# Feed-forward stage of a transformer layer on eight cores: weight blocks transposed one step ahead of their matmuls, and a down projection in 512 columns with a barrier in its loop

## The chip, the cores and the metric

The kernel runs on the 8 cores of one Trainium2 chip. The metric is the device time in microseconds (us) of the slowest core. The cores don't exchange anything: each has its own 1024 tokens and reads all weights itself.

## The reference

One transformer layer, pre-norm, on 8192 tokens of width 4096. The attention half has 32 query heads of 128 and one shared key and value head:

```python
def _silu(x):
    return jax.nn.silu(x)
def attn(x, wq, wk, wv, wo):          # x: 1 x 8192 x 4096
    q = (x @ wq).reshape(B, T, 32, 128)
    k = x @ wk
    v = x @ wv
    probs = softmax(causal(q @ k.T * scale))
    return (probs @ v).reshape(B, T, C) @ wo
def ffn(x, w_gate, s_gate, w_up, s_up, w_down, s_down):
    g = jnp.einsum('th,ih->ti', xt, w_gate.astype(x.dtype)) * s_gate   # i = 11008
    u = jnp.einsum('th,ih->ti', xt, w_up.astype(x.dtype)) * s_up
    h = jax.nn.silu(g) * u
    return jnp.einsum('ti,hi->th', h, w_down.astype(x.dtype)) * s_down
x = x + attn(layernorm(x), ...)
x = x + ffn(layernorm(x), ...)
```

The three feed-forward weights are int32 tables with values of -127 to 127, one scale for each row.

## The kernel before

A core owns eight tiles of 128 tokens (`OWN` = 1024 columns). It computes keys and values of all 64 tiles, its own queries, attention, the output projection with wo (line 645), the residual, and the second layer norm, whose transposed result lies in SBUF as `BUF`: 32 chunks of the hidden dimension, each 128 partitions by 1024 tokens. Then come the two stages that the change touches.

**F1, the gate and up projections (lines 695 to 785).** The inner dimension of 11008 is worked in `NI` = 86 blocks of 128. For each block the three weights (`mi` 0 gate, 1 up, 2 down) come in four pieces of 128 x 1024 (`cg`). For every piece:
- POOL issues a DMA that casts int32 to bf16 (`ldw`, line 716), into one of two buffers that each weight has for itself, `wbf_in[mi][cg % 2]`. It waits until the piece two before it of the same weight is transposed.
- TensorE transposes its eight 128 x 128 squares into one of two PSUM tiles, `pb` (line 723).
- VectorE copies that tile to SBUF (line 734), and frees it.
- For gate and up, TensorE multiplies at once by the eight chunks of `BUF`, in two halves of 512 tokens: 16 matmuls (line 749). Gate sums up in ps_a and up in ps_b. A down piece has no matmul: its transpose is only stored.

So TensorE has, in a row: transposes of a piece, a wait for their copy, 16 matmuls of that piece, transposes of the next. At the end of a block, one SyncE DMA stores the transposed down weight of 128 x 4096 in the DRAM tensor `wdt_s` (line 756), ScalarE does silu (762), VectorE multiplies (767) and copies the first 256 tokens to `h_res` (777), and the other 768 go to the DRAM tensor `h_sp` (783).

**F2, the down projection (lines 789 to 863).** The 1024 tokens are four groups of 256 (`GT`), worked in two passes of two groups. In a pass, for each of `NJ` = 32 output chunks, SyncE loads a strip of the transposed down weight, 128 x 86 x 128, in pieces of 256 bytes (line 816), into one of two buffers; it waits for the matmuls of two strips before. For each of the two groups come 86 matmuls of 256 columns (829), a scaling from PSUM (835), and for each of two token tiles: a transpose (844), a load of the residual `y_sp` by POOL (849), an addition (853) and a store of the output by POOL (858). POOL's queue is in order, and load and store alternate on it: the load of a tile's residual stands behind the store of the tile before. A strip has four such tiles in all, and the whole stage 256.

**What orders the work.** Each engine gets its instructions in the order in which the program adds them. `Prog` (lines 31 to 116) turns each dependency into a wait on a semaphore. `P.barrier` (line 51) adds a NO_OP on all five engines (line 113 in the trace) that waits for the last instruction of each engine and for the last DMA of each stream. In this kernel barriers stand only between stages, "endF1" and "final" among them.

Of the kernel before, what the change touches and what calls it, by code (L numbers as in the profile page):

```python
# [118 lines left out]
def build_nc(T=8192, I_FFN=11008):  # L119
# [5 lines left out]
    NG = max(1, OWN // 256)  # L125
    GT = OWN // NG
# [3 lines left out]
    def nch(p):  # L130
# [21 lines left out]
    d_hsp = (nc.dram_tensor("h_sp", [NI, 128, OWN - GT], BF16).ap()  # L152
             if NG > 1 else None)
# [6 lines left out]
    with ExitStack() as stk:  # L160
# [20 lines left out]
        def stat(slot):  # L181
# [521 lines left out]
        hres_cp = None  # L703
        for i in range(NI):
            ipar = i % 2
            gu_last = [[None] * NHALF, [None] * NHALF]
            wdtcgs = []
            for mi, dw in enumerate((d_wg, d_wu, d_wd)):
                for cg in range(4):
                    wpar = cg % 2  # L710
                    if mi < 2:
                        src = dw[i * 128:(i + 1) * 128, cg * 1024:(cg + 1) * 1024]
                    else:
                        src = dw.rearrange("(j q) c -> q j c", q=128)[
                            :, cg * 8:(cg + 1) * 8, i * 128:(i + 1) * 128]
                    ldw = dma("gp", wbf_in[mi][wpar], src,
                              deps=[win_rel.get((mi, wpar))], tag="wld",
                              stream=f"wl{mi}{wpar}")
                    pbp = (cg + mi) % 2
                    trs = []  # L720
                    for s in range(8):
                        trs.append(add("t", lambda e, s=s, mi=mi, wpar=wpar,
# [80 lines left out]
        for ipass, gset in enumerate(passes):  # L803
            hbuf = {}
            hloads = []
            for k, g in enumerate(gset):
                tgt = h_res if k == 0 else h_2nd
                hbuf[g] = tgt
                if ipass == 0 and k == 0:
                    continue  # L810
# [144 lines left out]
```

How the kernel before makes its waits and increments, by code:

```python
        def run_engine(handle, eng):  # L83
# [11 lines left out]
                    if (p["eng"] == eng and e_["fn"] is not None  # L95
                            and e_["sem"] == p["sem"]):
                        pass
                    sname = p["sem"]
                    if satisfied.get(sname, 0) >= p["val"]:
                        continue
                    waits[sname] = max(waits.get(sname, 0), p["val"])
                if eng in CHAIN_ENGS and prev_val is not None:
                    waits[eng] = max(waits.get(eng, 0), prev_val)
                for se, v in sorted(waits.items()):
                    handle.wait_ge(get_sem(se), v)
                    satisfied[se] = v
                if e_["fn"] is not None:
                    inst = e_["fn"](handle)
                    if e_["val"] is not None:
                        inst.then_inc(get_sem(e_["sem"]),
                                      16 if e_["sem"].startswith("D:") else 1)
                elif e_["val"] is not None:
                    handle.nop().then_inc(get_sem(e_["sem"]), 1)
```

## Time and profile before

| | us |
|---|---|
| median of 2 runs | 13707.56 |
| the two runs | 13509.33 and 13905.8 |
| the profiled execution, time | 13509.33 |
| its span, slowest core (core 1) | 13507.8 |
| spans of the eight cores | 13362.5 to 13507.8 |

The profiled execution is the faster of the two runs; 1.5 us of its time lie outside the span. The trace is that of core 1. F1 lies from 6762 to 11305 us of the span and F2 from 11305 to its end. PE is TensorE's matmuls (a transpose is one of them), PEld its weight loads, DVE VectorE, ACT ScalarE, SP SyncE.

### The profile page before, as it was taken

The numbers are of one execution on the slowest core, as the hardware profiler recorded it, in microseconds if no ns is written. First come the engines' busy times: TensorE is split into PE (matmuls) and PEld (weight loads), VectorE is DVE, ScalarE is ACT, GpSimd is POOL, SyncE is SP. The second block draws the span as 40 slices with busy tenths as digits, with TensorE's granted clock in tenths as the row PEclk, the third lists the DMA queues.
The fourth block names the chain that finished last, engine by engine and source line by source line (L and its number), as shares of the span: only waits on it lengthen the run. The fifth ranks groups of instructions, "written<-read, shape, count | busy, mean of one in ns | idle before, by whom it ended". The sixth has DMA issues, their size and how long they took to land.

```text
span 13507.8 us, 161305 instructions; the slowest of 8 cores (13362.5 to 13507.8 us)
## 1 busy us (share of the span) xinstructions
PE 8560.6 (63%) x62528; PEld 5506.4 (41%) x62528; DVE 4714.6 (35%) x8140; ACT 2398.4 (18%) x3696; POOL 1069.6 (8%) x1649
## 2 busy tenths in 40 slices
PE   3444675555655555678477777777767765665766
PEld 3443234444444444433233333333333333554655
DVE  4443117877777777720311111111111111000000
ACT  3443003444444444400100000000000000000000
POOL 0000000000000000000011111111111111111111
PEclk6666887888888888888588888888888888887888
DMA  3223660000000000067455555555555555544444
GB/s 119 113 113 112 106 106 1 1 1 1 1 1 1 1 1 1 1 72 91 145 86 81 82 86 82 81 86 81 82 86 81 82 85 104 107 101 113 103 103 96
DMA packets 1471353, 944.14 MB, mean 70 GB/s; under 512 B 1229296, under 2 KB 1338736, under 8 KB 1448336
## 3 DMA queue, kind: packets, MB, share of 16 engines
q0 software_dynamic: 683760, 423.86, 24.5%
q1 hardware_dynamic: 786848, 509.97, 12.4%
q8 instruction: 514, 8.42, 0.3%
q14 instruction: 231, 1.89, 0.1%
HBM read 1149.57 MB, written 157.42 MB: 97 GB/s over the span
## 4 chain that ended last, share of the span: by engine, by line
PE 41%; DMA 22%; DVE 21%; issue 8%; ACT 6%; POOL 1%; DVEq 1%; ACTq 0%; POOLq 0%; SPq 0%; PEldq 0%
DMA AR<-y_sp 12%; PE ps_a L749 11%; PE ps_b L749 9%; DVE AR L505 6%; DMA AR<-wd 4%; DVE AR L734 4%; PE pb L723 3%; ACT AR L518 3%; DVE AR L261 3%; PE pb L544 3%; PE ps_b L476 2%; ACT AR L276 2%; DMA AR<-wq 2%; PE pf_b L581 2%; PE pb L292 2%
## 5 line engine op out<-in xcount | busy, mean ns | idle before, releaser
L734 DVE COPY AR<-pb 128x1024 bf16<-128x1024 bf16 x1032 | 705.1, 690 | 3754.3 <-PE pb L723 3754.1
L749 PE MATMUL ps_a<-AR 128*128 128x512 bf16 x5504 | 1424.7, 418 | 386.4 <-DVE AR L734 386.4
L749 PE MATMUL ps_b<-AR 128*128 128x512 bf16 x5504 | 1243.0, 379 | 324.8 <-DVE AR L734 324.8
L476 PE MATMUL ps_b<-AR 128*128 128x512 bf16 x1152 | 428.4, 460 | 1107.8 <-ACT AR L518 632.0
L723 PE MATMUL pb<-AR 128*128 128x128 bf16 x8256 | 719.0, 241 | 607.1 <-DMA AR<-wd 549.8
L749 PEld LDWEIGHTS ps_a<-AR 128*128 128x128 bf16 x5504 | 555.9, 105 | 1153.0 <-issue 688.0
L544 PEld LDWEIGHTS pb<-AR 128*128 128x128 bf16 x9216 | 779.4, 116 | 435.6 <-issue 272.1
L723 PEld LDWEIGHTS pb<-AR 128*128 128x128 bf16 x8256 | 603.3, 108 | 822.7 <-issue 660.4
L292 PE MATMUL pb<-AR 128*128 128x128 bf16 x2560 | 292.8, 304 | 988.0 <-ACT AR L276 980.5
L544 PE MATMUL pb<-AR 128*128 128x128 bf16 x9216 | 889.1, 253 | 28.7 <-ACT AR L518 23.1
L762 ACT ACTIVATE AR<-ps_a,AR 128x512 f32<-128x512 f32 x172 | 118.2, 688 | 4419.4 <-PE ps_a L749 4330.9
L749 PEld LDWEIGHTS ps_b<-AR 128*128 128x128 bf16 x5504 | 513.7, 97 | 944.1 <-issue 374.5
L564 DVE COPY AR<-pb 128x1024 bf16<-128x1024 bf16 x1152 | 787.3, 683 | 1.2 <-issue 1.2
L476 PE MATMUL ps_a<-AR 128*128 128x512 bf16 x1152 | 440.0, 471 | 472.1 <-ACT AR L518 294.4
L829 PE MATMUL ps_b<-AR 128*128 128x256 bf16 x5504 | 735.2, 304 | 0.0
L829 PE MATMUL ps_a<-AR 128*128 128x256 bf16 x5504 | 645.1, 281 | 131.2 <-DMA AR<-h_sp 76.8
L292 PEld LDWEIGHTS pb<-AR 128*128 128x128 bf16 x2560 | 250.6, 138 | 1027.4 <-issue 1021.0
L829 PEld LDWEIGHTS ps_b<-AR 128*128 128x128 bf16 x5504 | 605.0, 110 | 125.0
L829 PEld LDWEIGHTS ps_a<-AR 128*128 128x128 bf16 x5504 | 556.0, 101 | 210.2 <-issue 131.6
L518 ACT ACTIVATE AR<-ps_a,AR 128x1024 bf16<-128x1024 f32 x576 | 632.4, 1098 | 1.3 <-issue 0.7
L518 ACT ACTIVATE AR<-ps_b,AR 128x1024 bf16<-128x1024 f32 x576 | 632.4, 1098 | 1.3 <-issue 1.1
L505 DVE TENSOR_REDUCE AR<-ps_b 128x1 f32<-128x1024 f32 x512 | 624.6, 1220 | 20.7 <-PE pb L544 1.5
(89 smaller groups left out, 9376.2 us busy)
## 6 DMA issues: line engine op xcount, KB each, us to landing
AR<-wdt_s SPq DMA_DIRECT2D x64, 2752.0 KB, 22.3
AR<-x SPq DMA_DIRECT2D x64, 2048.0 KB, 8.4
AR<-wg POOLq DMA_DIRECT2D x344, 256.0 KB, 6.4
AR<-wu POOLq DMA_DIRECT2D x344, 256.0 KB, 5.0
AR<-wd POOLq DMA_DIRECT2D x344, 256.0 KB, 5.8
wdt_s<-AR SPq DMA_DIRECT2D x86, 1024.0 KB, 4.0
AR<-wq POOLq DMA_DIRECT2D x64, 1024.0 KB, 9.6
AR<-xq SPq DMA_DIRECT2D x16, 2048.0 KB, 11.9
```

What stands on the lines that cost most here:

```text
L261: e1 = add("v", lambda e: e.reduce_sum(s_sum, src, axis=AX.X), deps_in, "ln_sum")
L276: e9 = add("s", lambda e: e.activation(dst_bf, src, AF.Identity, bias=s_negmr, scale=s_rstd), [e8], "ln_apply")
L292: e.transpose(p[:, s * 128:(s + 1) * 128], src_bf[:, j * 128:(j + 1) * 128], eye16),
L476: e.matmul(S[:, sh * 512:(sh + 1) * 512], BUF[:, h * OWN + p * 128: h * OWN + (p + 1) * 128], KT[:, n * 1024 + sh * 512: n * 1024 + (sh + ...
L505: rmx = add("v", lambda e, S=S, ph=ph: e.reduce_max(mtmp[ph], S[:, :], axis=AX.X, negate=True), ms_after + [mneg_last.get(ph)], "rmax")
L518: eev = add("s", lambda e, S=S, cp=cp, ph=ph: e.activation(p_sb[cp], S[:, :], AF.Exp, bias=mneg[ph]), ms_after + [bias_ready, p_rel.get(cp ...
L544: trs.append(add("t", lambda e, s=s, cp=cp: e.transpose(pb_t[cp][:, s * 128:(s + 1) * 128], p_sb[cp][:, s * 128:(s + 1) * 128], eye16), [r ...
L564: ptev = add("v", lambda e, cp=cp: e.tensor_copy(pt_sb[cp], pb_t[cp][:, :]), r["trs"] + [pts_rel.get(cp)], "ptev")
L723: pbp=pbp: e.transpose(pb_t[pbp][:, s * 128:(s + 1) * 128], wbf_in[mi][wpar][:, s * 128:(s + 1) * 128], eye16),
L734: tev = add("v", lambda e, dst=dst, pbp=pbp: e.tensor_copy(dst, pb_t[pbp][:, :]), trs + xd, "wtev")
L749: half=half, hp=hp: e.matmul(psg[mi][hp][:, 0:HT], wT[mi][wpar][:, s * 128:(s + 1) * 128], BUF[:, j * OWN + half * HT: j * OWN + (half + 1 ...
L829: e.matmul(psd[gp_], strip[sp][:, i * 128:(i + 1) * 128], hb[:, i * GT:(i + 1) * GT], start=(i == 0), stop=(i == NI - 1)), dep, "dmm")
```

## The change

Three things are done; nothing is changed ahead of F1.

1. **F1.** A piece's 16 matmuls are not added right behind its transposes but put in a list (`pending`), and are added once the next gate or up piece has been transposed. The work at a block's end (silu, multiply, copies, store) goes through the same list. The last up piece's matmuls therefore stand behind the four down pieces of transposes. The six input buffers, two for each weight, become four that all pieces go through in turn; the transposed pieces too have four. The transposed down weight is stored in four DMAs of 128 x 1024 out of two buffers, where it was one of 128 x 4096.
2. **F2.** A pass works one group of `GTP` = 512 tokens: 86 matmuls of 512 columns for a strip where there were twice 86 of 256. The number of strips, 64, and of token tiles, 256, stays. The second pass loads its 512 columns of `h_sp` in one DMA on SyncE's queue, where POOL loaded three parts of 256.
3. **The barrier "final"** has moved into the loop over the output chunks `j`: it is added 64 times, at the end of each.

```diff
-        for i in range(NI):
+        for i_ffn in range(NI):
...
-                    wpar = cg % 2
+                    buf = ub % 4
+                    ub += 1
...
-                    ldw = dma("gp", wbf_in[mi][wpar], src,
-                              deps=[win_rel.get((mi, wpar))], tag="wld",
-                              stream=f"wl{mi}{wpar}")
-                    pbp = (cg + mi) % 2
+                    ldw = dma("gp", wbf_in[buf], wsrc,
+                              deps=[win_rel.get(buf)], tag="wld",
+                              stream=f"wl{buf}")
+                    pbp = buf % 2
...
+                    if mi == 2:
+                        wd_dma = dma("sy", d_wdt[i, :, cg * 1024:(cg + 1) * 1024],
+                                     wdtcg[cg % 2], deps=[tev],
+                                     tag="wdtout", stream=f"wd{cg % 2}")
+                        wdt_rel[cg % 2] = wd_dma
                         continue
...
+                    def mk_mm(i=i, mi=mi, cg=cg, buf=buf, tev=tev,
+                              gu_last=gu_last):
...
+                    pending.append(mk_mm())
+                    flush()
...
-            wdt_dma = dma("sy", d_wdt[i], wdt_full[ipar], deps=wdtcgs,
-                          tag="wdtout", stream=f"wd{ipar}")
...
+            pending.append(mk_epi())
+            flush()
+        flush(0)
...
-        psd = [ps_a[:, 0:GT], ps_b[:, 0:GT]]
+        psd = [ps_a[:, 0:GTP], ps_b[:, 0:GTP]]
...
+        for ipass in range(NPASS):
+            hload = None
+            if ipass > 0:
+                hsrc = d_hsp.rearrange("i q c -> q i c")[
+                    :, :, (ipass - 1) * GTP: ipass * GTP]
+                hload = dma("sy", h_all, hsrc, deps=[pass_last], tag="hl",
+                            stream="hl")
             for j in range(NJ):
...
+                gp_ = j % 2
+                mm = None
+                for i in range(NI):
...
+                        psd[gp_], strip[sp][:, i * 128:(i + 1) * 128],
+                        h_all[:, i * GTP:(i + 1) * GTP],
+                        start=(i == 0), stop=(i == NI - 1)), dep, "dmm")
...
+                d_rel[gp_] = last_tr
+
+                P.barrier("final")
-        P.barrier("final")
```

`flush()` takes items from the head of `pending` and adds them until one is left.

How the instructions stand now. First TensorE in F1, from the third up piece of a block to the first gate pieces of the next. pb0 and pb1 are the two PSUM tiles of the transposes, ps_a and ps_b the sums of gate and up; x16 are the 16 matmuls of a piece. Before:

```order
L723 MATMUL pb1<-AR 128x128 x8
L749 MATMUL ps_b<-AR 128x512 x16
L723 MATMUL pb0<-AR 128x128 x8
L749 MATMUL ps_b<-AR 128x512 x16
L723 MATMUL pb0<-AR 128x128 x8
L723 MATMUL pb1<-AR 128x128 x8
L723 MATMUL pb0<-AR 128x128 x8
L723 MATMUL pb1<-AR 128x128 x8
L723 MATMUL pb0<-AR 128x128 x8
L749 MATMUL ps_a<-AR 128x512 x16
L723 MATMUL pb1<-AR 128x128 x8
L749 MATMUL ps_a<-AR 128x512 x16
```

The same place after the change:

```order
L731 MATMUL pb0<-AR 128x128 x8
L766 MATMUL ps_b<-AR 128x512 x16
L731 MATMUL pb1<-AR 128x128 x8
L766 MATMUL ps_b<-AR 128x512 x16
L731 MATMUL pb0<-AR 128x128 x8
L731 MATMUL pb1<-AR 128x128 x8
L731 MATMUL pb0<-AR 128x128 x8
L731 MATMUL pb1<-AR 128x128 x8
L766 MATMUL ps_b<-AR 128x512 x16
L731 MATMUL pb0<-AR 128x128 x8
L731 MATMUL pb1<-AR 128x128 x8
L766 MATMUL ps_a<-AR 128x512 x16
```

Each x16 row now belongs to the piece transposed one x8 row earlier than the row ahead of it, and the last of ps_b has moved behind the four down pieces.

Next TensorE in F2, one strip. st0 and st1 are the semaphores of the strip loads, sem_v VectorE's. Before:

```order
L829 MATMUL ps_a<-AR 128x256 [waits sem_D_sy_st0]
L829 MATMUL ps_a<-AR 128x256 x85
L844 MATMUL pf_a<-AR 128x128 [waits sem_v]
L844 MATMUL pf_b<-AR 128x128
L829 MATMUL ps_b<-AR 128x256 x86
L844 MATMUL pf_a<-AR 128x128 [waits sem_v]
L844 MATMUL pf_b<-AR 128x128
```

After, with the barrier's NO_OP; ow and yl are the semaphores of the output stores and of the residual loads:

```order
L847 MATMUL ps_a<-AR 128x512 [waits sem_D_sy_st0]
L847 MATMUL ps_a<-AR 128x512 x85
L862 MATMUL pf_a<-AR 128x128 [waits sem_v]
L862 MATMUL pf_b<-AR 128x128
L862 MATMUL pf_a<-AR 128x128 [waits sem_v]
L862 MATMUL pf_b<-AR 128x128 [waits sem_v]
L113 NO_OP [waits sem_D_gp_ow0,sem_D_gp_ow1,sem_D_gp_yl0,sem_D_gp_yl1,sem_s,sem_v]
```

One group of matmuls is left for a strip, four transposes follow it, and TensorE then waits until the last output store has landed.

Last SyncE, from the end of F1 into F2. Before:

```order
L240 DMA wdt_s<-AR 128x4096 [waits sem_D_sy_wd1,sem_v]
L240 DMA h_sp<-AR 128x768 [waits sem_D_sy_hs1,sem_v]
L113 NO_OP [waits sem_D_gp_wl00,sem_D_gp_wl01,sem_D_gp_wl10,sem_D_gp_wl11,sem_D_gp_wl20,sem_D_gp_wl21,sem_D_sy_hs0,sem_D_sy_hs1,sem_D_sy_wd0,sem_D_sy_wd1,sem_s,sem_t,sem_v]
L240 DMA AR<-wdt_s 128x86x128 x2
L240 DMA AR<-wdt_s 128x86x128 [waits sem_D_sy_st0,sem_t]
L240 DMA AR<-wdt_s 128x86x128 [waits sem_D_sy_st1,sem_t]
```

After:

```order
L239 DMA wdt_s<-AR 128x1024 [waits sem_D_sy_wd1,sem_v]
L239 DMA h_sp<-AR 128x512 [waits sem_D_sy_hs1,sem_v]
L113 NO_OP [waits sem_D_gp_wl0,sem_D_gp_wl1,sem_D_gp_wl2,sem_D_gp_wl3,sem_D_sy_hs0,sem_D_sy_hs1,sem_D_sy_wd0,sem_D_sy_wd1,sem_s,sem_t,sem_v]
L239 DMA AR<-wdt_s 128x86x128
L113 NO_OP [waits sem_D_gp_ow0,sem_D_gp_ow1,sem_D_gp_yl0,sem_D_gp_yl1,sem_D_sy_st0,sem_s,sem_t,sem_v]
L239 DMA AR<-wdt_s 128x86x128
L113 NO_OP [waits sem_D_gp_ow0,sem_D_gp_ow1,sem_D_gp_yl0,sem_D_gp_yl1,sem_D_sy_st1,sem_s,sem_t,sem_v]
```

Two strips were in hand at a time. Now the load of each strip stands behind a NO_OP that waits for everything of the strip before it.

## Rows read from the trace of the kernel before

**Rows 1.** The page's chain of waits: shares of the span by line.
```profile
DMA AR<-y_sp 12%; PE ps_a L749 11%; PE ps_b L749 9%; DVE AR L505 6%; DMA AR<-wd 4%; DVE AR L734 4%; PE pb L723 3%; ACT AR L518 3%; DVE AR L261 3%; PE pb L544 3%; PE ps_b L476 2%; ACT AR L276 2%; DMA AR<-wq 2%; PE pf_b L581 2%; PE pb L292 2%
```
**Rows 2.** Busy time in stretches: F1, then F2; the columns in the first line.
```profile
core 1: us, PE busy (x) PEld busy (x) DVE busy (x) ACT busy (x) POOL busy (x), PEclk, DMA share, GB/s
6762.00:11305.00 4543.00, 3236.94 (x19040) 1653.57 (x19040) 823.25 (x1279) 116.97 (x170) 662.88 (x1018) 0.88 0.53 83
...
11305.00:13508.00 2203.00, 1426.37 (x11264) 1189.78 (x11264) 129.25 (x384) 0.00 (x0) 284.56 (x515) 0.80 0.48 106
```
**Rows 3.** The waits in F1: who waited for whom, total us, times, longest.
```profile
PE pb L723 <- DMA AR<-wd: 544.0, 162, 7.1
PE ps_a L749 <- DVE AR L734: 382.6, 340, 2.0
...
PE ps_b L749 <- DVE AR L734: 321.1, 340, 0.9
```
**Rows 4.** Timeline of one block of F1: start, us, instruction, idle before it.
```profile
9007.48 6.24 PE L749 MATMUL ps_a<-AR 128*128 128x512 bf16 x16 [1.71 <-DVE AR L734]
...
9015.11 3.61 PE L749 MATMUL ps_a<-AR 128*128 128x512 bf16 x16 [0.94 <-DVE AR L734]
...
9018.56 0.61 PE L723 MATMUL pb<-AR 128*128 128x128 bf16 x8
...
9049.74 1.75 POOL L240 DMA_DIRECT2D AR<-wd  x2 [12.71 <-PE pb L723]
...
9054.77 1.01 PE L723 MATMUL pb<-AR 128*128 128x128 bf16 x8 [5.13 <-DMA AR<-wd]
```
**Rows 5.** The page's DMA issues: KB each, median us from issue to landing.
```profile
AR<-wdt_s SPq DMA_DIRECT2D x64, 2752.0 KB, 22.3
...
wdt_s<-AR SPq DMA_DIRECT2D x86, 1024.0 KB, 4.0
...
out<-AR POOLq DMA_DIRECT2D x256, 64.0 KB, 3.7
```
**Rows 6.** Timeline of F2: its first strip, then one residual load to the next.
```profile
11351.76 12.47 PE L829 MATMUL ps_a<-AR 128*128 128x256 bf16 x86 [54.42 <-DMA AR<-wdt_s]
11364.34 0.48 DVE L835 TENSOR_SCALAR AR<-ps_a,AR 128x256 f32<-128x256 f32 x1 [64.56 <-PE ps_a L829]
...
11365.22 9.55 PE L829 MATMUL ps_b<-AR 128*128 128x256 bf16 x86
...
11365.38 0.29 DVE L853 TENSOR_TENSOR AR<-pf_a,AR 128x128 f32<-128x128 f32 x1 [0.56 <-PE pf_b L844]
...
11856.56 0.29 DVE L853 TENSOR_TENSOR AR<-pf_a,AR 128x128 f32<-128x128 f32 x1 [5.81 <-DMA AR<-y_sp]
11857.42 0.54 POOL L240 DMA_DIRECT2D out<-AR  x1 [5.42 <-DVE AR L853]
11857.96 0.54 POOL L240 DMA_DIRECT2D AR<-y_sp  x1
11861.76 0.29 DVE L853 TENSOR_TENSOR AR<-pf_b,AR 128x128 f32<-128x128 f32 x1 [4.91 <-DMA AR<-y_sp]
```
**Rows 7.** All instructions on y_sp in F2: us to landing.
```profile
DMA to landing us min/median/max: 2.0/5.2/37.1
```
**Rows 8.** Busy time in 4 us of F2 while a strip is loaded.
```profile
11840.00:11844.00 4.00, 3.55 (x33) 2.94 (x30) 0.00 (x0) 0.00 (x0) 0.00 (x0) 1.00 1.01 229
```
**Rows 9.** The chain of waits: one of the two h_sp loads before pass two.
```profile
12427.64 25.50 DMA AR<-h_sp
```
**Rows 10.** The chain in the wo projection: two groups of 32 matmuls.
```profile
6095.78 8.42 PE ps_b L645 x32
...
6249.14 7.07 PE ps_a L645 x32
```
**Rows 11.** Busy time in 80 us of it, core 1, then core 2.
```profile
6091.00:6171.00 80.00, 75.44 (x283) 30.43 (x281) 6.23 (x9) 0.00 (x0) 6.70 (x4) 0.80 0.86 91
...
6091.00:6171.00 80.00, 71.56 (x326) 31.95 (x331) 6.91 (x10) 0.00 (x0) 8.38 (x5) 1.00 0.95 108
```

More of the change, by code:

```diff
@@ L740, in build_nc, with mk_epi, emit @@
+                    pending.append(mk_mm())
+                    flush()
+            def mk_epi(i=i, ipar=ipar, gu_last=gu_last):
+                def emit():
+                    nonlocal_state = None
+                    hlast = None
                     for half in range(NHALF):
                         hp = half % 2
[L742 to L753 removed]
@@ L802, in build_nc @@
         pass_last = None
[L803 to L810, printed above, removed]
-                src = d_hsp.rearrange("i q c -> q i c")[
-                    :, :, (g - 1) * GT: g * GT]
-                hloads.append(dma("gp", tgt, src, deps=[pass_last], tag=f"hl{g}", stream="hl"))
+        for ipass in range(NPASS):
[5 more added lines that the diff above has]
+                            stream="hl")
             for j in range(NJ):
@@ new lines, in build_nc @@
+                strip_rel[sp] = mm
+                pass_last = mm
+                dev = add("v", lambda e, j=j, gp_=gp_: e.tensor_scalar_mul(
+                    dscr[gp_], psd[gp_], sd_sb[:, j:j + 1]),
+                    [mm, ld_sd, d_rel.get(gp_)], "dscl")
+                psd_rel[gp_] = dev
+                last_tr = None
+                for tt in range(GTP // 128):
+                    ptile = ipass * (GTP // 128) + tt
+                    fp = (j * (GTP // 128) + tt) % 2
+                    tr = add("t", lambda e, tt=tt, gp_=gp_, fp=fp:
+                             e.transpose(
+                        pf2[fp][:, 0:128],
+                        dscr[gp_][:, tt * 128:(tt + 1) * 128], eye32),
+                        [dev, ld_eye32, pf3_rel.get(fp)], "dtr")
+                    last_tr = tr
+                    yld = dma("gp", yscr[fp],
+                              d_ysp[ptile, :, j * 128:(j + 1) * 128],
+                              deps=[y_rel.get(fp)], tag="yld",
+                              stream=f"yl{fp}")
+                    oev = add("v", lambda e, fp=fp: e.tensor_tensor(
+                        oscr[fp], pf2[fp][:, 0:128], yscr[fp], ALU.add),
+                        [tr, yld, orel.get(fp)], "oadd")
+                    pf3_rel[fp] = oev
+                    y_rel[fp] = oev
+                    od = dma("gp", d_out[ptile, :, j * 128:(j + 1) * 128],
+                             oscr[fp], deps=[oev], tag="outw",
+                             stream=f"ow{fp}")
+                    orel[fp] = od
```

214 lines of the change are left out of this document (91 added, 123 removed).

## The prediction

> **What bounds the kernel now.** I read the chain of waits first, since the page's busy shares mix stages with different limits. Its costliest line is the residual load from y_sp in F2, 12% of the span, with the matmuls of F1 (L749) and its loads and copies (wd, L734) behind it [rows 1]. The change touches F1 and F2 alone, so I then took the two stretches: F1 is 4543 us, 52.8 for each of its 86 blocks, with TensorE busy 71%, and F2 is 2203 us, 34.4 for each of 64 strips [rows 2].
>
> In F1 the waits of TensorE name three things: down pieces that have not landed, 544.0 us; and VectorE's copy of the transposes ahead of the matmuls, 382.6 + 321.1 us [rows 3]. The timeline of one block shows both. After a piece's transposes TensorE idles 0.94 us until the copy is there, then works 3.61 us on 16 matmuls. Among the down pieces it idles 5.13 us for a load, and after that the first 16 matmuls take 6.24 us instead of 3.61: the granted clock is then at its lower level, half speed [rows 4].
>
> In F2 nothing on TensorE is the bound. The chain runs from one residual load to the next through POOL's queue. With little other traffic, one addition follows the last after 5.2 us (11856.56 to 11861.76) [rows 6]; four of these would be 21 us, but a strip takes 34.4, because the 64 KB transfers share the DMA engines with the strips: their landing ranges from 2.0 to 37.1 us [rows 7]. The strip's own 22.3 us [rows 5] lie beside this work today, since the next strip is always loaded ahead.
>
> **The change in F1.** With the transposes one piece ahead, the copy lies beside 16 matmuls and the 0.94 us wait goes, on all 8 pieces of a block. From the start of 16 matmuls to the next transposes are 3.45 us (9015.11 to 9018.56), and the transposes take 0.61 [rows 4]: 4.06 for a piece, 32.5 for eight. The four down pieces: 4 x 0.61 = 2.4, and 0.5 where the third and fourth wait for a copy, because there are two PSUM tiles. New is that the copy of the third down piece waits until the store of the first has landed, 4.0 us for 1 MB [rows 5], here 256 KB. Behind it stand the copies of the next gate pieces on VectorE. The last up piece's 3.45 us of matmuls cover most of that; I take 0.7 (bounds 0, if the small store lands in 2.5 us, and 4 if nothing covers it). Sum: 36.1 us a block, 3105 in all.
>
> Are the loads in time? A down piece lands 5.0 us after its issue (9049.74 to 9054.77) [rows 4]. The fourth is now issued once the last up piece is transposed. Then come 3.45 us of matmuls and three groups of transposes with their waits, some 6 us together. So it just lands in time, and the others earlier. The DMA engines were busy 0.53 of 52.8 us [rows 2], 28 us of work for a block; in 36.1 us that is 0.78. It fits, with little to spare. The cold start of 2.6 us for a block goes with the wait.
>
> Clock. All this is at the full clock, 1.00 or 2.4 GHz. The wo projection, where TensorE is as dense as F1 will be, shows another value: 0.80 on core 1 over 80 us, and in it 32 matmuls took 8.42 us instead of 7.07 [rows 10, 11]. It lies between the two levels of 1.2 and 2.4 GHz. Core 2 has 1.00 in the same 80 us [rows 11]. At that clock 16 matmuls are 4.2 us, a piece 4.95, a block 43.7, F1 3758 us. Nothing in the trace says how much of the new F1 will have it. I take half: 39.9 us a block, 3431 us. F1 then gains 1112 us, with bounds 785 and 1438.
>
> The Trainium skill (TensorE: Matmul & The Clock Gate, Part 1, the note on the peak-current limiter) says that a whole die goes to 13/16 of its clock once three of its cores run dense matmuls, and stays there while the load lasts. The trace differs in that core 1 had it and core 2 of its die did not [rows 11]. By the page all of F1 would be at 13/16, and the total would be that of the third case below.
>
> **The change in F2.** The matmul work stays: 86 x 512 columns for twice 86 x 256. What changes the stage is the barrier. SyncE's NO_OP waits for the last output store, and behind it stands the load of the next strip; TensorE's stands ahead of the next matmuls, POOL's ahead of the next residual load. The load, the matmuls and the four tiles, side by side before, now come one after the other. One round:
> - barrier and issue, 0.4 us (an estimate; signals between engines cost 0.1 to 0.6 in rows 6);
> - strip from issue to landing: 22.3 median [rows 5], with residual loads beside it. Alone I take 21.0;
> - matmuls: 3.45 / 16 = 0.216 us each, 18.7 for 86. After a round's wait the clock is at its lower level: 86 matmuls took 12.47 us after a long wait and 9.55 warm, 2.9 more [rows 6]. I take 2.5, so 21.2, and 0.2 to VectorE;
> - scaling of 512 columns: 0.48 for 256 [rows 6], at most 0.96, taken 0.8; transpose and hops up to the first addition 0.56 (11364.82 to 11365.38). Together 1.4;
> - three more tiles at 5.2 = 15.6. The first residual load lies beside the strip, the three others can't, since POOL's queue has each behind a store;
> - the last store is issued 0.9 us after its addition (11856.56 to 11857.42) [rows 6] and lands 3.0 later (3.7 median with strips beside it [rows 5]).
>
> Sum 63.7 us, 4077 for 64 rounds. The second pass's load of h_sp, twice what took 25.50 us [rows 9], stands ahead of a strip on the same queue: 50 more. F2 becomes 4127 us, 1924 longer. Bounds for a round: 54 (strip 16, tile cycle 4.0, cold start 1.5) and 74 (strip 25, tile cycle 7, last store 5), so F2 grows by 1300 to 2580.
>
> **Sum.** 13507.8 - 4543 + 3431 - 2203 + 4127 = 14319.8, and with the 1.5 us outside the span 14321; I say 14320. That is 6.0% over the profiled execution, 4.5% over the median, which holds a run of 13905.8. The time is meant against the undisturbed 13509.
>
> **Rivals.**
> *Full clock in F1.* Blocks of 36.1 us: 326 less, 13995. For it: in F1 before, the clock is 1.00 whenever it is warm. Against: rows 10 and 11.
> *F1 wins less: 0.81 throughout, or loads that come late.* The first gives 14321 + 327 = 14648. The second: four shared buffers leave the last down piece about 1 us of slack, with DMA engines at 0.78; if each block keeps its 5.13 us wait and the cold 2.6, that is 662 more than at full clock, 14657. The two prices are the same, so they are one case. Then the edit in F1 does only in part what it says.
> *Not slower: transfers alone run at their floor.* After the barrier no strip disturbs the residual loads, and they don't disturb the strip. In F2 the DMA engines reached 229 GB/s [rows 8]: at that rate 2.8 MB take 12.3 us, 14.5 with the ends, and a residual load lands in 2.0 instead of 3.8 [rows 7]. A round is shorter by 6.5 + 3 x 1.8 = 11.9 us, 762 in all: 13233 at full clock, 13559 at half. It decides the sign if a round is below 60.3 us at full clock, or 55.2 at half. Against: the load is made of 256-byte pieces and seldom reached this rate, and its 22.3 us are a median over rounds in which it was mostly alone with one small transfer.
> The Trainium skill (DMA: Bandwidth & Descriptors, Bandwidth) gives 6.15 us for 1 MB, and says in the same section that descriptors of 256 bytes lose speed to a fixed cost. By its rate the strip would be an estimated 17 us, which would take 4 us off a round. No row here shows a strip that fast.
>
> **How the numbers follow.** The forecast has 0.40, full clock in F1 0.25, little gain in F1 0.17, transfers at their floor 0.12, and 0.06 is left for rounds over 70 us. All but the fourth are slower; a measurement of this kernel can tell about 2% from no change, so up to 13780 counts as the same. Of the fourth I give 0.03 to faster and 0.09 to same, and 0.01 more to same for a round just under 60 us at full clock. Slower has 0.87. The range reaches from the middle of the fourth case, 13650, to 14950, which is past the third with rounds of 68 us.
>
> **What would show it.** F1's stretch at 3100 to 3760 us, no wait of L766 for VectorE's copy, almost none for wd. F2's at 4000 to 4250, with the wait of TensorE for wdt_s near 64 x 40 us (strip and tiles both lie in it), SyncE's queue waiting for out, and 16 us from the first to the last addition of a round. The chain should carry wdt_s as its largest DMA, which it does not hold today [rows 1]. I am wrong if a round is below 56 us, or if F1 stays above 3900.

## The result, and the profile after

| | before | after |
|---|---|---|
| median, us | 13649.45 (13 runs) | 14157.72 (14 runs) |
| lowest and highest | 13479.97, 13949.34 | 13771.96, 14408.9 |
| profiled execution | 13509.33 | 14094.02 |
| span of core 1 in it | 13507.8 | 13711.5 |

The changed kernel is slower: the ratio is 1.019, with a 95% interval of 1.010 to 1.028. So it is slower, but whether by more than 2% the interval leaves open. The sign and the range held, but the forecast said 6.0% over an undisturbed execution, and 1.9% was measured. In many executions the cores of one die show a lower granted clock and take 200 to 600 us longer; the ratio is taken without those, and so all stages below are read on core 1, whose die was not among the slow ones in either profiled execution.

The stages are cut alike in both traces: F1 from its first transpose to its last matmul, F2 from there to the end. Cut so, F1 of before begins at 6711 us and ends at 11289; the forecast was made from stretches that begin at 6762 and 11305, hence its 4543 and 2203 us where the table has 4578 and 2219.

| core 1, us | before | after | change | forecast |
|---|---|---|---|---|
| ahead of F1 | 6711 | 6571 | -140 | 0 |
| F1 | 4578 | 3372 | -1206 | -1112 |
| F2 | 2219 | 3769 | +1550 | +1924 |

The first row holds no edit. Cores 2 to 7 of before began F1 at 6592 to 6640 us, and over all profiled executions here cores began it at 6552 to 6740. The 140 us are thus a difference between two executions: core 1 began late in the one and early in the other. The forecast, which was made against the span of the first, took them along. Its error of 608 us on core 1 (14319.8 against 13711.5) is thus 140 + 94 from F1 + 374 from F2.

The chain of waits of the changed kernel (slowest core, 6), which answers to [rows 1]. wdt_s is now its largest DMA, y_sp has gone from 12% to 3%, and the store of wdt_s is new, with 4%:

```profile
PE ps_a L766 10%; DMA AR<-wdt_s 9%; PE ps_b L766 7%; DVE AR L504 6%; PE ps_b L847 5%; PE ps_a L847 5%; DMA wdt_s<-AR 4%; DMA AR<-y_sp 3%; PE pb L731 3%; ACT AR L517 3%; DVE AR L260 2%; PE pb L543 2%; PE ps_b L475 2%; ACT AR L275 2%; PE pf_b L580 2%
```

Busy time of the two stretches on core 1, against [rows 2]. In F1 TensorE went from 71% busy to 89% and its clock from 0.88 to 0.97. In F2 it went down to 38% of the stretch, at a clock of 0.67, and the DMA engines from 0.48 to 0.25. The stage moves nearly the same bytes in 1.7 times the time:

```profile
core 1: us, PE busy (x) PEld busy (x) DVE busy (x) ACT busy (x) POOL busy (x), PEclk, DMA share, GB/s
6572.00:9953.00 3381.00, 3000.16 (x19256) 1570.77 (x19256) 829.69 (x1290) 119.39 (x173) 668.07 (x1029) 0.97 0.77 111
9953.00:13711.00 3758.00, 1418.70 (x5760) 602.61 (x5760) 122.69 (x320) 0.00 (x0) 273.96 (x511) 0.67 0.25 60
```

**F1 after.** The waits of core 1 in F1, against [rows 3] (who waited for whom: us in total, times, longest):

```profile
DVE AR L742 <- DMA wdt_s<-AR: 546.8, 148, 8.4
PE pb L731 <- DVE AR L742: 273.2, 231, 4.8
PE pb L731 <- DMA AR<-wd: 85.7, 68, 3.3
...
PE ps_a L766 <- DVE AR L742: 3.1, 7, 0.5
```

The wait of the matmuls for VectorE's copy went from 703.7 us to 3.1, and that for down pieces from 544.0 to 85.7. In their place VectorE waits 546.8 us for stores of wdt_s, and TensorE's transposes 273.2 us for VectorE. The timeline of one block's end on core 1 shows how (start, us, instruction, idle before it):

```profile
8006.29 0.61 PE L731 MATMUL pb<-AR 128*128 128x128 bf16 x8
8006.73 3.62 PE L766 MATMUL ps_b<-AR 128*128 128x512 bf16 x16
...
8011.68 8.65 SPq L239 DMA_DIRECT2D wdt_s<-AR  x4
...
8012.81 3.62 PE L766 MATMUL ps_b<-AR 128*128 128x512 bf16 x16
...
8016.85 0.69 DVE L742 COPY AR<-pb 128x1024 bf16<-128x1024 bf16 x1 [4.66 <-DMA wdt_s<-AR]
8017.68 0.61 PE L731 MATMUL pb<-AR 128*128 128x128 bf16 x8 [1.25 <-DVE AR L742]
...
8019.23 1.29 DVE L742 COPY AR<-pb 128x1024 bf16<-128x1024 bf16 x2 [1.70 <-DMA wdt_s<-AR]
8020.07 1.01 PE L731 MATMUL pb<-AR 128*128 128x128 bf16 x8 [1.78 <-DVE AR L742]
8020.88 6.15 PE L766 MATMUL ps_a<-AR 128*128 128x512 bf16 x16
```

The copy of the third down piece waits 4.66 us, since the store of the first has not landed, and the fourth waits 1.70. With both PSUM tiles taken TensorE, done with the last up piece's matmuls at 8016.43, idles 1.25 and then 1.78 us. The next 16 matmuls then take 6.15 us instead of 3.62. A store of 256 KB lands after 6.0 us here (median of 344 in F1). A block takes 39.2 us.

**F2 after.** The waits of core 1 in F2, and one whole round:

```profile
PE ps_a L847 <- DMA AR<-wdt_s: 981.7, 32, 65.0
PE ps_b L847 <- DMA AR<-wdt_s: 950.0, 32, 32.2
DVE AR L871 <- DMA AR<-y_sp: 753.5, 192, 6.3
```

```profile
11999.85 0.29 DVE L871 TENSOR_TENSOR AR<-pf_a,AR 128x128 f32<-128x128 f32 x1 [0.55 <-PE pf_b L862]
...
12005.34 0.29 DVE L871 TENSOR_TENSOR AR<-pf_b,AR 128x128 f32<-128x128 f32 x1 [5.19 <-DMA AR<-y_sp]
...
12009.23 0.29 DVE L871 TENSOR_TENSOR AR<-pf_a,AR 128x128 f32<-128x128 f32 x1 [3.60 <-DMA AR<-y_sp]
...
12013.03 0.29 DVE L871 TENSOR_TENSOR AR<-pf_b,AR 128x128 f32<-128x128 f32 x1 [3.51 <-DMA AR<-y_sp]
12013.90 0.54 POOL L239 DMA_DIRECT2D out<-AR  x1 [2.73 <-DVE AR L871]
12016.16 0.36 SPq L239 DMA_DIRECT2D AR<-wdt_s  x1
...
12035.67 20.87 PE L847 MATMUL ps_b<-AR 128*128 128x512 bf16 x86 [29.45 <-DMA AR<-wdt_s]
12056.65 0.75 DVE L853 TENSOR_SCALAR AR<-ps_b,AR 128x512 f32<-128x512 f32 x1 [43.33 <-PE ps_b L847]
...
12057.96 0.29 DVE L871 TENSOR_TENSOR AR<-pf_a,AR 128x128 f32<-128x128 f32 x1 [0.56 <-PE pf_b L862]
```

Read it by its differences. Four additions are 13.2 us apart (11999.85 to 12013.03), and the last store goes out 0.87 later. SyncE issues the strip 2.26 us after that, the strip lands after 19.5, the matmuls take 20.87, and 1.42 us later comes the next first addition. That makes 58.1 us; the mean over the stage, with the load of h_sp in it, is 58.9. The DMA issues of this stretch (KB each, median us to landing), against [rows 5]:

```profile
AR<-wdt_s SPq DMA_DIRECT2D x63, 2752.0 KB, 19.6
out<-AR POOLq DMA_DIRECT2D x256, 64.0 KB, 1.8
AR<-y_sp POOLq DMA_DIRECT2D x255, 64.0 KB, 2.3
AR<-h_sp SPq DMA_DIRECT2D x1, 11008.0 KB, 35.2
```

### The profile page after: what moved, and what is told of

Same layout as the page of the kernel before. It is cut to its first block, busy times and chain, and to the rows that moved or that the text cites. A ratio compares the mean times of both kernels' runs of the same rounds, so it can differ in the third digit from the quotient of the medians.

```text
span 14092.4 us, 153803 instructions; the slowest of 8 cores (13711.5 to 14092.4 us)
## 1 busy us (share of the span) xinstructions
PE 8693.3 (62%) x57024; PEld 4962.7 (35%) x57024; DVE 4706.8 (33%) x8076; ACT 2395.9 (17%) x3696; POOL 1061.2 (8%) x1646
## 4 chain that ended last, share of the span: by engine, by line
PE 48%; DMA 21%; DVE 17%; ACT 6%; issue 6%; POOL 1%; DVEq 1%; another core or an unknown queue 1%; ACTq 0%; POOLq 0%; SPq 0%; PEldq 0%
PE ps_a L766 10%; DMA AR<-wdt_s 9%; PE ps_b L766 7%; DVE AR L504 6%; PE ps_b L847 5%; PE ps_a L847 5%; DMA wdt_s<-AR 4%; DMA AR<-y_sp 3%; PE pb L731 3%; ACT AR L517 3%; DVE AR L260 2%; PE pb L543 2%; PE ps_b L475 2%; ACT AR L275 2%; PE pf_b L580 2%
## 5 line engine op out<-in xcount | busy, mean ns | idle before, releaser
L766 PE MATMUL ps_a<-AR 128*128 128x512 bf16 x5504 | 1471.9, 429 | 0.3 <-DVE AR L742 0.3
L766 PE MATMUL ps_b<-AR 128*128 128x512 bf16 x5504 | 1375.9, 408 | 0.0
L847 PE MATMUL ps_a<-AR 128*128 128x512 bf16 x2752 | 667.0, 408 | 1000.9 <-DMA AR<-wdt_s 1000.9
L847 PE MATMUL ps_b<-AR 128*128 128x512 bf16 x2752 | 668.4, 409 | 971.4 <-DMA AR<-wdt_s 971.4
L475 PE MATMUL ps_b<-AR 128*128 128x512 bf16 x1152 | 436.1, 468 | 1114.0 <-ACT AR L517 576.0
L543 PEld LDWEIGHTS pb<-AR 128*128 128x128 bf16 x9216 | 786.8, 117 | 447.9 <-issue 303.4
L543 PE MATMUL pb<-AR 128*128 128x128 bf16 x9216 | 896.4, 254 | 29.5 <-ACT AR L517 22.5
L291 PE MATMUL pb<-AR 128*128 128x128 bf16 x2560 | 293.7, 304 | 979.5 <-ACT AR L275 971.9
L731 PE MATMUL pb<-AR 128*128 128x128 bf16 x8256 | 670.2, 232 | 322.2 <-DVE AR L742 290.3
L766 PEld LDWEIGHTS ps_a<-AR 128*128 128x128 bf16 x5504 | 579.1, 108 | 732.8 <-issue 465.7
L766 PEld LDWEIGHTS ps_b<-AR 128*128 128x128 bf16 x5504 | 554.4, 103 | 655.7 <-issue 368.4
L847 PEld LDWEIGHTS ps_a<-AR 128*128 128x128 bf16 x2752 | 283.2, 104 | 1378.5 <-issue 1100.3
L731 PEld LDWEIGHTS pb<-AR 128*128 128x128 bf16 x8256 | 566.9, 104 | 564.9 <-issue 484.7
L847 PEld LDWEIGHTS ps_b<-AR 128*128 128x128 bf16 x2752 | 283.6, 104 | 1349.8 <-issue 1072.5
L475 PE MATMUL ps_a<-AR 128*128 128x512 bf16 x1152 | 448.3, 479 | 456.3 <-ACT AR L517 284.1
L291 PEld LDWEIGHTS pb<-AR 128*128 128x128 bf16 x2560 | 251.4, 139 | 1019.3 <-issue 1012.8
```

What stands on the lines that cost most here:

```text
L291: e.transpose(p[:, s * 128:(s + 1) * 128], src_bf[:, j * 128:(j + 1) * 128], eye16),
L475: e.matmul(S[:, sh * 512:(sh + 1) * 512], BUF[:, h * OWN + p * 128: h * OWN + (p + 1) * 128], KT[:, n * 1024 + sh * 512: n * 1024 + (sh + ...
L543: trs.append(add("t", lambda e, s=s, cp=cp: e.transpose(pb_t[cp][:, s * 128:(s + 1) * 128], p_sb[cp][:, s * 128:(s + 1) * 128], eye16), [r ...
L731: e.transpose(pb_t[pbp][:, s * 128:(s + 1) * 128], wbf_in[buf][:, s * 128:(s + 1) * 128], eye16),
L766: e.matmul(psg[mi][hp][:, 0:HT], wT[buf][:, s * 128:(s + 1) * 128], BUF[:, j * OWN + half * HT: j * OWN + (half + 1) * HT], start=(j == 0) ...
L847: mm = add("t", lambda e, i=i, sp=sp, gp_=gp_: e.matmul(psd[gp_], strip[sp][:, i * 128:(i + 1) * 128], h_all[:, i * GTP:(i + 1) * GTP], st ...
```

## The experiments

### Where F2's 1550 us come from

**The changed kernel with the barrier behind the loops.**

```diff
-                P.barrier("final")
+        P.barrier("final")
```

> The changed kernel with its barrier moved back behind both loops; nothing else differs. Theory B (the barrier puts strip load, matmuls and tiles of a strip in a row, 20 + 21 + 17 us, and this is the whole loss of F2): a strip falls from 58.5 us to what the chain of residual loads allows beside strip loads, 33 to 35 us as before the change, F2 from 3758 us to 2100 to 2250, the time to 12,100 to 12,300 us, and landing of a residual load rises again from 2.3 us to about 5. Rival M (the groups of 512 columns are what costs, because four tiles hang on one group of matmuls): a strip stays above 45 us, F2 above 2900 and the time above 12,900. Rival S (with 512 columns the strip load alone would set the pace): F2 near 64 x 22 = 1400 us, time 11,400.

Measured: median 12414.89 us (4 runs), ratio to before 0.919 (95% 0.905 to 0.934). F1 stays at 39.0 us a block on core 1. F2 of core 1 is 2375 us, 37.1 a strip. The barrier in the loop so costs 3769 - 2375 = 1394 of the 1550 us. The other 156 were not expected: a strip takes 2.4 to 3.8 us more than on the same core before. The DMA issues of F2, core 1:

```profile
AR<-wdt_s SPq DMA_DIRECT2D x62, 2752.0 KB, 20.5
out<-AR POOLq DMA_DIRECT2D x256, 64.0 KB, 4.2
AR<-y_sp POOLq DMA_DIRECT2D x255, 64.0 KB, 4.9
AR<-h_sp SPq DMA_DIRECT2D x1, 11008.0 KB, 51.2
```

Against the rows after, this shows what the barrier gives back: with strips beside it a residual load takes 4.9 us instead of 2.3, an output store 4.2 instead of 1.8.

**The kernel before with the barrier inside the loop**, the same edit the other way.

> The kernel before with only its last barrier moved into the loop over the output chunks. Theory B: a strip becomes 0.4 + 20 (strip load) + 12 + 9.5 (two groups of 86 matmuls of 256 columns; the first group's two tiles lie beside the second group) + about 9 (scaling, last two tiles, last store) = 51 us, so F2 is 64 x 51 + 60 = 3320 us for 2203, and the time 13,509 + 1120 = 14,630 us; shorter by some 7 us a strip than the changed kernel's 58.5 because half of the tiles stay beside matmuls. Rival M (512 columns cost, the barrier little): less than 400 us over the kernel before, 13,900 or under.

Measured: median 14780.24 us (4 runs), profiled 14516.03. F2 is 3363 us, 52.5 a round: the barrier alone costs 1144. With groups of 512 a round is 58.9. So the two edits of F2 don't add up: the grouping costs 156 us without the barrier and 406 with it (3769 - 3363). The timeline tells the difference:

```profile
12517.56 50.54 SPq L240 DMA_DIRECT2D AR<-wdt_s  x2
...
12537.32 11.91 PE L829 MATMUL ps_a<-AR 128*128 128x256 bf16 x86 [27.33 <-DMA AR<-wdt_s]
...
12550.22 9.55 PE L829 MATMUL ps_b<-AR 128*128 128x256 bf16 x86
12550.38 0.29 DVE L853 TENSOR_TENSOR AR<-pf_a,AR 128x128 f32<-128x128 f32 x1 [0.55 <-PE pf_b L844]
```

With two groups the first addition comes 13.1 us after the strip (12537.32 to 12550.38), and two tiles lie beside the second group's matmuls. With one group it comes after 22.3 (12035.67 to 12057.96), and all four tiles stand behind the matmuls.

**The first experiment with two groups of 256 again**, to see whether the grouping makes those 156 us.

```diff
-                gp_ = j % 2
+                for k in range(2):
+                    gp_ = k
...
-                        psd[gp_], strip[sp][:, i * 128:(i + 1) * 128],
-                        h_all[:, i * GTP:(i + 1) * GTP],
+                            psd[gp_][:, 0:256],
+                            strip[sp][:, i * 128:(i + 1) * 128],
+                            h_all[:, i * GTP + k * 256:
+                                  i * GTP + (k + 1) * 256],
```

> The run with the barrier behind the loops, but with two groups of 86 matmuls of 256 columns for a strip, as in the kernel before, two tiles behind each. With groups of 512 and no barrier F2 took 37 to 38 us a strip where the kernel before took 34.5. Theory G (behind one group of 512, TensorE's second and fourth transpose wait on the chain of residual loads and hold the next matmuls up, and with two groups this wait halves): a strip returns to 34.3 to 35.0 us, F2 to 2200 to 2240, 150 to 200 us less. Rival N (the columns do nothing, the difference is h_sp on SyncE's queue or one chip's draw): F2 stays at 2350 to 2450.

Measured: 12308.53 us (12216.69 and 12400.37), F2 2175 to 2192 us, 34.2 a strip. The grouping it is. VectorE waits 1820.1 us for residual loads there (core 2), so POOL's queue is still the bound, and the likely reason is how early in a strip its first tiles are free. The run changes the number of groups and the columns of a matmul together, so it doesn't tell these two apart.

### What the barrier's chain is made of

**Four residual buffers, all four loads issued ahead of the matmuls; the barrier stays.**

```diff
+                ylds = []
+                for tt in range(GTP // 128):
+                    ylds.append(dma("gp", yscr[tt],
...
-                        [tr, yld, orel.get(fp)], "oadd")
+                        [tr, ylds[tt], orel.get(fp)], "oadd")
```

> The changed kernel, barrier in the loop and all, with four buffers for the residual y_sp, whose four loads are issued ahead of a strip's matmuls instead of one behind each store. Theory B prices the tiles in a round at about 13.1 us from the first addition to the last (5.4 + 3.9 + 3.8) because of those loads: now only a store's landing is between (the output scratch keeps its two buffers), about 3.4 us. A round falls from 58.5 to about 49 us, F2 by 620 us to about 3140. Rival P (POOL's issues and the store, not the residual loads, set the 13 us): a round falls by under 4 us.

Measured: 13494.69 us (13492.98 and 13496.4). F2 of core 1 falls from 3769 to 3215 us, 50.2 a round. The four additions now lie within 4.5 us (12024.75 to 12029.29) instead of 13.2, and what they still wait for is the store of the tile two before:

```profile
12027.94 0.29 DVE L874 TENSOR_TENSOR AR<-pf_a,AR 128x128 f32<-128x128 f32 x1 [2.70 <-DMA out<-AR]
```

The 8.7 us that a round loses are those by which the additions moved together: of the tiles' 13.2 us, 8.7 were the latency of three residual loads in a row.

**The next strip issued ahead of the barrier**, so that only the tiles stay behind it.

```diff
+                nxt = ld_strip(j + 1) if j + 1 < NJ else None
...
-                lds = dma("sy", strip[sp],
+                lds = ld_strip(0) if j == 0 else nxt
```

> The changed kernel with the barrier in the loop, but the load of strip j + 1 is issued right behind the matmuls of strip j in program order, so on SyncE ahead of the barrier that ends round j; it lands beside the matmuls of round j. Theory B: the strip's 20 us leave the row and everything else in it stays, a round is 38 to 39 us (matmuls 20.5 or a little less if TensorE restarts warmer, tiles 17), F2 about 2500 us, time 12,500 to 12,600. Rival C (the barrier's own signals and what waits on five engines cost several us a round): a round stays above 42 us.

Measured: 12975.75 us (12846.96 and 13104.54), F2 2801 to 2846 us, 43.8 a round on core 2. The direction was right, but 5 us less was won than expected, and the round lies where the rival of costly barrier signals had it, above 42. The timeline speaks against that rival: the last store is taken at 12020.63 and the next strip issued at 12023.26, 2.63 us with the store's landing in them, where the changed kernel has 2.26. The tiles are what is longer. The landing of a residual load is again that of the kernel with strips beside it (core 2, F2):

```profile
AR<-y_sp POOLq DMA_DIRECT2D x255, 64.0 KB, 4.3
```

Yet the core's own strip had landed before the slow tiles began: its four additions took 15.1 us (12004.70 to 12019.77), and from 12008 to 12020 its own DMA engines were only 0.15 to 0.26 busy. The strips of other cores may be what they met. No run tells that apart, and it stays open.

### What holds F1 at 39 us a block

**Four buffers for the transposed down pieces.**

```diff
-        wdtcg = [bbuf(F1B + 16384 + b * 2048, 1024) for b in range(2)]
+        wdtcg = [bbuf(3072 + b * 2048, 1024) for b in range(4)]
...
-                        dst = wdtcg[cg % 2]
-                        xd = [wdt_rel.get(cg % 2)]
+                        dst = wdtcg[cg]
+                        xd = [wdt_rel.get(cg)]
```

> The changed kernel with four SBUF buffers for the transposed down pieces where it has two (they lie where the key and value weights were), so that no copy waits for a store of the same block. Theory W (in F1 the copies that wait for these stores hold TensorE at each block's end, and the cold restart follows from it): F1 goes from 39.3 us a block to 36.1 to 36.6, 3381 to 3110 to 3150 us, the wait of L742 for wdt_s from 547 us to under 30, the 16 matmuls after the down pieces from 6.15 to 3.6 us, and the time falls by about 250 us. Rival D (DMA engines at 0.77 busy are the next bound): waits for wd and wg take its place, F1 stays above 3280 us and the DMA share does not pass 0.80.

Measured: median 13891.27 us (4 runs), lowest 13725.52. VectorE's wait for wdt_s went, but F1 gained only 1.1 us a block on core 1 (38.1). The waits in F1 say why:

```profile
PE pb L731 <- DMA AR<-wg: 117.1, 94, 6.3
...
PE pb L731 <- DMA AR<-wd: 84.9, 68, 2.6
PE pb L731 <- DVE AR L742: 57.8, 103, 1.0
```

TensorE's wait for the copies fell from 273.2 to 57.8 us, and loads of gate pieces came up from 8.0 to 117.1: with TensorE sooner at each load, the loads are next. That is nearly what the rival of busy DMA engines had forecast (F1 is 3279 us, the DMA share 0.78); the next run tells the buffers from the engines.

**The same with eight load buffers.**

```diff
-        wbf_in = [bbuf(F1B + b * 2048, 1024) for b in range(4)]
+        wbf_in = ([bbuf(F1B + b * 2048, 1024) for b in range(4)]
+                  + [bbuf(11264 + b * 2048, 1024) for b in range(4)])
...
-                    ldw = dma("gp", wbf_in[buf], wsrc,
-                              deps=[win_rel.get(buf)], tag="wld",
+                    ib = (ub - 1) % 8
+                    ldw = dma("gp", wbf_in[ib], wsrc,
+                              deps=[win_rel.get(ib)], tag="wld",
```

> The run with four store buffers in F1, and now also eight instead of four buffers for the weight loads. With four store buffers a block took 38.1 us, not 36.1 to 36.6, and TensorE waited 117 us for gate loads and 85 us for down loads. Theory L (the loads are late because a buffer's next load can only be issued four pieces ahead, and the DMA engines, at 0.77 busy, could deliver in time): these two waits fall under 40 us together, a block is 36.2 to 36.8 us, F1 3110 to 3170 us. Rival D (the DMA engines' throughput is the bound, whatever is queued): waits for loads stay above 120 us, F1 above 3220.

Measured: median 13845.1 us (4 runs), profiled 13513.86. Blocks of 36.6 us on cores 0 and 1, whose granted clock from 7000 to 9500 us was 0.93, 34.8 to 35.6 on the others at 0.98 and 0.99, and the waits for loads are gone (0.2 us on core 1). So the DMA engines can deliver in time, once the loads are issued earlier. On core 1 store buffers alone gave 1.1 us a block; both edits together gave 2.6 there at the lower clock and 4.4 at best; load buffers alone were not run. 2500 us of F1 on core 4, with TensorE 97% busy:

```profile
7000.00:9500.00 2500.00, 2428.34 (x16086) 1295.94 (x16084) 693.83 (x1078) 97.56 (x142) 559.39 (x862) 0.99 0.90 125
```

### A version that beats both

**No barrier in the loop, four buffers for down pieces, four residual buffers with early loads** (the edits of three experiments above together).

> The changed kernel with the barrier behind the loops, four residual buffers loaded ahead, and four buffers for the transposed down pieces. If B and W hold and nothing new comes up, a strip takes 18.7 us of matmuls and 2 to 3 us of scaling and transposes, 21 to 22 us, F2 about 1450 us; F1 3110 to 3150; time 11,100 to 11,300 us, under both kernels. Rival S: the strip load, 20 us alone, takes 24 us or more beside the small transfers and sets the pace: F2 above 1600 us, time above 11,400, and TensorE waits for wdt_s at each strip.

Measured: median 11930.92 us (4 runs), lowest 11704.57. F2 takes 27.3 to 28.8 us a strip, 6 more than expected, at the length the rival of slow strips had, though not by its wait: TensorE waited for wdt_s only twice. With the residual loads early, VectorE waits for the output stores instead: 920.1 us in 84 waits on core 1. Beside strips that now follow each other with little pause, small and large transfers are late (DMA issues of F2, core 1):

```profile
AR<-wdt_s SPq DMA_DIRECT2D x62, 2752.0 KB, 29.1
out<-AR POOLq DMA_DIRECT2D x254, 64.0 KB, 11.4
```

**Eight load buffers too, and for each strip one residual load, one addition and one store of 256 KB instead of four.**

```diff
+                oev = add("v", lambda e, gp_=gp_: e.tensor_tensor(
+                    oscr[gp_], pf2[gp_][:, 0:GTP], yscr[gp_], ALU.add),
+                    [last_tr, yld, orel.get(gp_)], "oadd")
```

> Barrier behind the loops; four store and eight load buffers in F1; and in F2 one load of the residual (256 KB, a strip ahead), four transposes into one PSUM tile, one addition of 512 columns and one store for a strip, so that 2 small transfers are in flight where there were 8. The run with eight small transfers took 27.3 to 28.8 us a strip, because additions waited 923 us for stores that landed 11.4 us late and the strips themselves took 29.1 us. If that was the small transfers' doing: 18.7 of matmuls + 1.0 for the scaling + 0.6 of transposes = 20.5 to 22 us a strip, F2 1350 to 1450, F1 3110 to 3170, time 11,050 to 11,250 us. Rival S (strip loads back to back set the pace, whatever the small ones are): TensorE waits for wdt_s at most strips, a strip above 24 us, time above 11,350.

Measured: median 11702.71 us (4 runs), lowest 11375.9. F1 has 34.5 us a block on all eight cores. F2 stays at 27.3 us a strip, though the waits for stores are gone. So fewer transfers alone won nothing in F2, and the expected 20.5 to 22 us a strip were missed. Now TensorE waits for strips, as the rival had it, and a strip takes 31.9 us to land (median). The waits of core 1 in the last 1524 us of F2:

```profile
PE ps_b L856 <- DMA AR<-wdt_s: 186.0, 28, 12.6
PE ps_a L856 <- DMA AR<-wdt_s: 110.4, 21, 66.6
```

**The same with wdt_s laid out by output chunk**, so that a strip is read as one contiguous 22 KB for each partition, and the stores of F1 are written in pieces of 256 bytes instead.

```diff
-    d_wdt = nc.dram_tensor("wdt_s", [NI, 128, D], BF16).ap()
+    d_wdt = nc.dram_tensor("wdt_s", [NJ, 128, NI * 128], BF16).ap()
...
-                          d_wdt.rearrange("i q c -> q i c")[
-                              :, :, j * 128:(j + 1) * 128],
+                          d_wdt[j],
```

> The run with one addition for a strip, with one more edit: wdt_s is laid out by strip, so that F1 writes it in pieces of 256 bytes and F2 reads each strip in 22 KB a partition, where F1 wrote 2 KB and F2 read 256 bytes. That run took 27.3 us a strip, with TensorE waiting for wdt_s and a strip landing in 31.9 us. Theory K (the 256-byte pieces of the strip reads set that pace): a strip lands in under 15 us, TensorE waits for it only at the two starts, a strip takes 20.4 to 21.5 us, F2 1350 to 1420. F1, whose DMA engines are 0.84 busy, pays with some of it: its 344 writes become 1024 pieces each, F1 2970 to 3250 us; time 11,000 to 11,300. Rival H (the memory, shared by the cores, is the limit whatever the pieces): a strip stays above 25 us.

Measured: median 11336.15 us (6 runs), lowest 10942.98. On cores 2 to 7 F2 is 1360 to 1366 us, 21.3 a strip, and F1 is unchanged at 34.5, so the short writes cost it nothing there. Cores 0 and 1, at a granted clock of 0.91 in F1, had 37.3 us a block and 23.4 a strip. Core 4 in F2, first its DMA issues, then the timeline:

```profile
AR<-wdt_s SPq DMA_DIRECT2D x60, 2752.0 KB, 11.8
```

```profile
10104.17 18.73 PE L859 MATMUL ps_b<-AR 128*128 128x512 bf16 x86
...
10124.37 18.73 PE L859 MATMUL ps_a<-AR 128*128 128x512 bf16 x86
```

One strip begins 20.2 us after the last, 18.7 of them matmuls: F2 is bound by TensorE, and this version's lowest run stands at 0.80 of the lowest run of before beside it (13597.65).

## Why the prediction was right in sign and too large

**Right.** That the barrier turns three things that lay side by side into a chain, and that this outweighs all that F1 gains: shown by moving the barrier alone, both ways (+1144 in the kernel before, -1394 in the changed one, where F1 gains 1206). That the order of transposes in F1 removes the wait of L766. The first and last terms of a round (barrier and strip issue, matmuls at 21.2 against 20.87, hops at 1.4 against 1.42) held, and the strip of 21.0 against 19.5 nearly.

**Wrong: the step "three more tiles at 5.2 = 15.6".** They took 13.2 in the round shown, and at the end of it the last store was taken at 3.0 us and landed in 1.8. The pair of additions I read in [rows 6], 5.2 us apart, came from a moment that I called one with little other traffic. For this core's own DMA engines it was one (the last two figures of each row, busy share and GB/s, core 1 of before):

```profile
11855.00:11859.00 4.00, 4.00 (x33) 3.40 (x32) 0.29 (x1) 0.00 (x0) 1.07 (x2) 0.86 0.08 21
11859.00:11862.00 3.00, 3.00 (x30) 2.69 (x29) 0.24 (x1) 0.00 (x0) 0.00 (x0) 1.00 0.22 22
```

With the barrier a residual load lands in 2.3 us and a cycle is 3.8; only the first cycle behind the matmuls is 5.5. So a core that loads no strip itself saw both lengths, here and in the run with the strip issued ahead of the barrier. Strips of the other cores are the likely difference, since behind a barrier each core loads one for only 19.6 of 58.9 us, but no run shows it.

Together tiles 2.4, store 1.2 and strip 1.5 are 5.1 of the 5.6 us by which a round of 58.1 lies under the forecast 63.7; 64 of them are 358 of the 374 us, and the h_sp load, 35 us where 50 was allowed for, is the rest. No single term carries the forecast's 608 us: over 64 rounds the tiles are 154 of them, the strip 96 and the store 77, and F1's 94 and the 140 ahead of it come on top. The signs named for F2 missed with the same terms: the stage is 3769 us, not 4000 to 4250, TensorE waited 1932 us for wdt_s, not 64 x 40, and 13.2 us lie between first and last addition, not 16.

I had the mechanism as a rival, "transfers alone run at their floor", and gave it 0.12. Of its two prices one was right (small transfers: 2.3 where it said 2.0), the other was not: a strip alone takes 19.6 us, not 14.5, since when it is alone on its core the layout of its source sets its speed. The last experiment shows that: contiguous, it lands in 11.8. (The 3.8 us of that rival's residual load are not in [rows 7], whose median is 5.2; they are the step from 11857.96 to 11861.76 in [rows 6].)

**F1: a total that was nearly right for a wrong reason.** I forecast 39.9 us a block, as the mean of 36.1 at full clock and 43.7 at 0.81. Core 1 has 39.2, but no stretch at 0.81: over every 100 us of F1 its clock was 0.93 or more, 0.97 in the mean, which is full but for the cold restarts. That the two came out alike is luck. (Core 6 of the same execution was at 0.77 to 0.92 up to 9200 us; it took 42.1.)

The failed steps are three. The piece was 4.06 and is 3.90 (8002.39, the transposes ahead of those shown, to 8006.29), since the next matmuls begin 0.44 us behind the start of the transposes and not 0.61; that takes 1.3 us off a block, and without the 0.7 the forecast's sum would be 34.1. The versions with eight load buffers have 34.5 to 34.8 where the clock is 0.99 or 1.00. "I take 0.7" for the copy behind the store was far too little: in the block shown it costs 1.25 + 1.78 us of waiting and 2.53 of cold restart, and the wait alone is 273.2 us in 86 blocks. And of the fourth down piece "it just lands in time" did not hold once the stores were out of the way: four store buffers alone gave back only 1.1 of the 4.7 us between 34.5 and 39.2, because TensorE then waited for loads. Store and load waits lie behind one another, and the runs don't divide the 4.7 us between them.

I took the store's landing as 4.0 us from one of 1 MB in a stage where the DMA engines were 0.53 busy. At 0.77 busy a quarter of the bytes takes 6.0. The rival "full clock" was right about the clock and, with its 36.1, wrong about the block. That loads come late, the other rival, cost little as long as the stores held TensorE back (85.7 us for down pieces where it kept 5.13 a block), and more once they did not (202 us for gate and down pieces).

**A part not in the forecast.** 140 us of the span ahead of F1 differed between the two executions. A sum made against one execution's slowest core takes along what was particular to that core; the stage's starts on the other seven cores were there to be read.

## What to carry to other kernels

A barrier in a loop costs what it stops from overlapping, less what the transfers win by running alone, so price it with latencies taken where nothing else moves. A wait for a store's landing that looks covered may not be, once the change itself makes the DMA engines busier (here 6.0 us for 256 KB at a share of 0.77, where 1 MB had taken 4.0 at 0.53); and the idle time it leaves is paid twice, since TensorE starts again at its lower clock (6.15 us for 3.62). Where a stage waits on many small things in one queue, more buffers move the wait to the next of them (residual load, store, strip). Fewer transfers moved it once more, with no gain in F2; what ended it here was, on top of them, a layout that the hot read finds contiguous. The layout by itself was not run.

## What was not expected of the hardware

**Layout against neighbours.** The same 2752 KB took 19.6 us in 256-byte pieces with nothing of its own core beside it, 29.1 to 31.9 with strips nearly back to back, and 11.8 in one piece of 22 KB for each partition, with 256 KB transfers beside it. The Trainium skill (DMA: Bandwidth & Descriptors, "Why small descriptors are slow") puts the loss of a 256-byte piece at 27% of the bus's cycles. The direction agrees; the loss measured here, 19.6 against 11.8, is larger than that. The layout changed the length of the pieces and the distance between them at once, and no run separates the two.

**The clock under dense work.** With TensorE 96 to 97% busy in F1 on all eight cores the granted clock was full, as core 1 of the version with one addition shows:

```profile
7000.00:9500.00 2500.00, 2427.65 (x16240) 1300.17 (x16239) 700.40 (x1088) 100.31 (x146) 564.58 (x870) 1.00 0.85 127
```

In other executions of much the same F1 pairs of cores had less: 0.93 and 0.91 over this stretch on cores 0 and 1 of the first run with eight load buffers and of the one with the new layout, and 0.84 on core 6 of the changed kernel, where F1 took 42.1 us a block instead of core 1's 39.2:

```profile
7000.00:9500.00 2500.00, 2297.31 (x13042) 1152.48 (x13041) 563.17 (x877) 79.73 (x116) 454.47 (x699) 0.84 0.70 102
```

The Trainium skill (TensorE: Matmul & The Clock Gate, Part 1, the note on the peak-current limiter) says that three cores of a die with dense matmuls bring the die to 13/16. The first row speaks against it as a rule: all four cores of each die had TensorE busy for 2411 us or more of these 2500, at 1.00. What decides between the two rows no run here shows.
